# First pair of a two-stage graph kernel: loads in halves, hop 2 in float32, and a reordered end

## What is computed

```python
# first layer
Xw = X @ Wv + bv
sj, si = Xw @ aw[:d, 0], Xw @ aw[d:, 0]
e = leaky_relu(sj[:, None, :] + si[:, :, None] + ab[0], 0.2)
alpha = A * exp(e)
transition = alpha / (sum(alpha, -1, keepdims=True) + 1e-12)
H = 0; Xk = X
for k in range(3):
    H = H + Xk @ Wk[k] + bk[k]
    Xk = transition @ Xk
x = layernorm(x + relu(H))
# second layer
x = layernorm(x + (adj @ x) @ w)
```

## Time and profile before

| what | value |
|---|---|
| median of 3 runs | 272.70 us (272.46 to 272.84) |
| the profiled execution's own time | 272.39 us |
| its span, first to last instruction | 270.6 us |
| TensorE busy (PE) | 264.1 us, 98% |
| TensorE weight loads (PEld) | 246.1 us, 91% |
| VectorE (DVE), ScalarE (ACT), GpSimd (POOL) | 216.7, 193.0, 191.5 us |
| DMA | 34.91 MB, 129 GB/s in the mean |

### The profile page before, as it was taken

One profiled execution on the slowest core, in us unless ns is written; L12 is line 12 of the kernel. 1 busy time (PEld: TensorE's weight loads), 2 busy tenths in 40 slices (PEclk: granted clock), 3 DMA queues, 4 the chain that ended last, 5 costly groups with the idle time before them and its releaser, 6 DMA issues.

```text
span 270.6 us, 6025 instructions
## 1 busy us (share of the span) xinstructions
PE 264.1 (98%) x1890; PEld 246.1 (91%) x1890; DVE 216.7 (80%) x615; ACT 193.0 (71%) x439; POOL 191.5 (71%) x412
## 2 busy tenths in 40 slices
PE   8899999999999999999999999999999999999992
PEld 5899999999999999999999999999999999999991
DVE  0777798888889888888988888988888898788984
ACT  4887767777666777766777766677776667766874
POOL 4665567778877778887777887777788777657533
PEclk9999999999999999999999999999999999999999
DMA  7997486828955488446873484943884457932214
GB/s 242 274 185 94 85 48 218 131 72 147 168 137 159 81 133 117 155 143 156 140 117 80 154 155 137 152 153 51 131 160 100 118 116 75 125 99 78 80 41 155
DMA packets 28342, 34.91 MB, mean 129 GB/s; under 512 B 6803, under 2 KB 16150, under 8 KB 28310
## 3 DMA queue, kind: packets, MB, share of 16 engines
q1 hardware_dynamic: 27888, 34.12, 60.8%
q10 hardware_dynamic: 422, 0.40, 0.4%
HBM read 26.09 MB, written 8.42 MB: 128 GB/s over the span
## 4 chain that ended last, share of the span: by engine, by line
PE 95%; DMA 2%; DVE 1%; SPq 0%; ACT 0%; issue 0%
PE ps_v L1107 31%; PE ps_y L1107 17%; PE ps_out L1107 15%; PE ps_h L1107 11%; PE ps_agg L1271 10%; PE ps_v L1204 3%; PE ps_v L1208 3%; PE ps_v L1206 3%; DMA WY_sb<-Wk_dram 2%; PE ps_agg L1107 2%; DVE last_out_sb L884 0%; PE ps_v L1254 0%; PE ps_h L1245 0%; PE ps_y L1245 0%; PE ps_agg L1254 0%; DVE WY_lo L669 0%
## 5 line engine op out<-in xcount | busy, mean ns | idle before, releaser
L1107 PE MATMUL ps_v<-WX_hi,XT_hi 128*128 128x512 f32 (+1 forms) x132 | 49.0, 371 | 0.0
L1107 PE MATMUL ps_v<-WX_lo,XT_hi 128*128 128x512 f32 (+1 forms) x132 | 48.6, 368 | 0.0
L1107 PE MATMUL ps_v<-WX_hi,XT_lo 128*128 128x512 f32 (+1 forms) x132 | 48.6, 368 | 0.0
L1029 POOL TENSOR_TENSOR XT_lo<-xt,XT_hi 128x512 fp32r<-128x512 f32 x32 | 42.1, 1319 | 6.6 <-ACT XT_hi L426 6.6
L1039 POOL TENSOR_TENSOR alpha<-exps,adjs 128x256 f32<-128x256 f32 x31 | 23.1, 744 | 28.9 <-ACT exps L470 28.8
L1043 POOL TENSOR_TENSOR alpha_lo<-alpha,alpha_hi 128x256 fp32r<-128x256 f32 x31 | 22.8, 735 | 19.4 <-ACT alpha_hi L479 19.4
L1107 PE MATMUL ps_y<-WY_hi,XT_hi 128*128 128x258 f32 x116 | 35.2, 303 | 0.6 <-DVE WY_lo L673 0.6
L503 ACT ACTIVATE y<-res,offset,rstd 128x256 f32<-128x256 f32 x62 | 33.6, 591 | 2.2 <-POOL offset L1005 2.2
L1271 PEld LDWEIGHTS ps_agg<-adjs,y 128*128 128x128 f32 x248 | 32.0, 191 | 2.2
L1271 PE MATMUL ps_agg<-adjs,y 128*128 128x128 f32 x248 | 32.7, 275 | 0.0
L1107 PE MATMUL ps_y<-WY_lo,XT_hi 128*128 128x258 f32 x116 | 32.7, 282 | 0.0
(11 more groups left out here) (179 smaller groups left out, 830.8 us busy)
## 6 DMA issues: line engine op xcount, KB each, us to landing
xt<-xt_dram SPq DMA_DIRECT2D x32, 256.0 KB, 5.7
nodes<-nodes_dram SPq DMA_DIRECT2D x32, 256.0 KB, 5.8
out_dram<-out_sb SPq DMA_DIRECT2D x30, 256.0 KB, 5.3
adjs<-adjs_dram SPq DMA_DIRECT2D x32, 128.0 KB, 5.7
spread<-si_rows_dram SPq DMA_DIRECT2D x29, 128.0 KB, 4.7
si_rows_dram<-scores SPq DMA_DIRECT2D x29, 1.0 KB, 3.9
WvT_sb<-WvT_dram SPq DMA_DIRECT2D x1, 260.0 KB, 3.6
W_sb<-Wk_dram ACTq DMA_DIRECT2D x1, 256.0 KB, 3.3
```

What stands on the lines that cost most here:

```text
L1029: pool.tensor_tensor(XT_lo[k % 7][:].rearrange("p c b i -> p (c b i)"), xt_sb[k % 4][:], XT_hi[k % 7][:].rearrange("p c b i -> p (c b i)") ...
L1107: last = pe.matmul(to, a, b, start=start and n == 0, stop=stop and n == 2, skip_group_check=True)
```

## The change

- X0 and W0 are loaded in two halves each (by chunk of 128 features), with semaphores of their own; first hop 0 goes by chunk instead of by graph, so that it can begin with the first halves. One warm-up product fewer.
- Hop 2 of pair 0 is a whole float32 product of X0 and WY_sb, which has room for the two score columns (`first_hop2`). It waits for W2 and for the columns' copy (`u_ready`), and no longer for high and low parts. `load_xt(4)` waits for it.
- Score weights come behind all of first hop 0, then the sum of biases, which uses ps_v, then the score shift. bk is rounded first on ScalarE's list.
- Hop 2 of pair 1 (`second_hop2`) does the products with X1's high part first, and only then waits for its low part. One graph of hop 2 of pair 2 is moved ahead of `propagate_v2(0)`.
- VectorE's preamble: score columns, bias copy, score shift, low part of W1, low part of W2 with its two columns in one instruction, low part of W0.
- W1, W2 (258 columns) and w lie by partition in DRAM, with runs of 2 KB.
- At the end: the first half of pair 31 is stored ahead of the half of pair 30; the root of graph 0 is taken between the two halves of `late_normalise2(LAST - 2)`; the reciprocal of graph 0 comes ahead of the moments of graph 1.

```diff
@@ SyncE
-                    sp.wait_ge(h_done, 1)
+                    sp.wait_ge(y_done, 1)
...
-            load_xt(0)
+            half = C * PER * P // 2
+            sp.dma_start(xt_sb[0][:, 0:half], xt[0, :, 0:half]).then_inc(first_xt_loaded, DMA)
+            sp.dma_start(xt_sb[0][:, half:2 * half], xt[0, :, half:2 * half]).then_inc(xt_loaded[0], DMA)
...
+            store_last(0)
             sp.wait_ge(late_half_out_ready, 1)
             sp.dma_start(out[LAST - 1, :, 0:D], out_sb[(LAST - 1) % 3][:, 0]).then_inc(last_stored, DMA)
-            for b in range(PER):
-                sp.wait_ge(last_out_ready, b + 1)
-                sp.dma_start(out[LAST, :, b * D:(b + 1) * D], last_out_sb[:, b]).then_inc(last_stored, DMA)
+            store_last(1)
@@ ScalarE
-            act.dma_start(W0_sb[:], Wk[0].rearrange("(c p) n -> p c n", p=P)).then_inc(Wk_loaded[0], DMA)
+            act.dma_start(W0_sb[:, 0], W0[:, 0:D]).then_inc(first_W0_loaded, DMA)
+            act.dma_start(W0_sb[:, 1], W0[:, D:2 * D]).then_inc(Wk_loaded[0], DMA)
...
+            bk_hi_of()
             xt_hi(0)
             wx_hi(0)
             wy_hi()
             wx_hi(1)
-            bk_hi_of()
...
-            late_normalise2(LAST - 2)
+            late_normalise2(LAST - 2, [0])
             last_std2_of(0)
+            late_normalise2(LAST - 2, [1])
@@ VectorE
+            def score_columns():
+                dve.wait_ge(Wk_loaded[2], DMA)
+                dve.wait_ge(u_done, 1)
+                dve.tensor_copy(WY_sb[:, :, D:D + 2], ps_u).then_inc(u_ready, 1)
+                dve.tensor_copy(WY_hi[:, :, D:D + 2], ps_u).then_inc(u_ready, 1)
...
             bk_lo_of()
+            score_columns()
+            bias_of_hops()
             shift_of_scores()
+            first_hop1_low()
+            wy_lo()
             first_hop0_low()
...
+            last_rstd2_of(0)
             last_mom2(1)
-            for b in range(PER):
-                last_normalise2(b)
+            last_normalise2(0)
+            last_rstd2_of(1)
+            last_normalise2(1)
@@ TensorE
+            def first_hop2():
+                pe.wait_ge(Wk_loaded[2], DMA)
+                pe.wait_ge(u_ready, 1)
+                for b in range(PER):
+                    for c in range(C):
+                        last = pe.matmul(hop2(0)[:, b, 0:D + 2], first_X[:, c, b], WY_sb[:, c], start=c == 0,
+                                         stop=c == C - 1, skip_group_check=True)
+                last.then_inc(y_done, 1)
...
-            keep_warm(ps_v[:, 0], 8)
+            keep_warm(ps_v[:, 0], 7)
             first_hop0(0)
+            first_hop0(1)
             score_weights()
-            first_hop0(1)
+            sum_of_biases()
             score_shift()
-            hop2_and_scores(0)
+            first_hop2()
             first_hop1(0)
             pe.wait_ge(identity_ready, 1)
             spread_scores(0)
             first_hop1(1)
-            hop2_and_scores(1)
-            sum_of_biases()
+            second_hop2()
+            hop2_and_scores(2, [0])
             pe.wait_ge(ones_columns_ready, 1)
             propagate_v2(0)
             spread_scores(1)
-            hop2_and_scores(2)
+            hop2_and_scores(2, [1])
             hop2_and_scores(3)
             spread_scores(2)
```

More of the change, by code:

```diff
@@ L16, with resnorm_graph_kernel @@
 NORM_EPS = 1e-5
-def resnorm_graph_kernel(nc, xt, adjs, nodes, WvT, Wk, bk, w, si_rows, out):
+def resnorm_graph_kernel(nc, xt, adjs, nodes, WvT, W0, W1, W2, bk, w, si_rows, out):
     PAIRS = nodes.shape[0]
-    D = w.shape[0]
+    D = bk.shape[1]
     C = D // P
-    HOPS = Wk.shape[0]
+    HOPS = bk.shape[0]
     assert (P, C, HOPS) == (nodes.shape[1], 2, 3)
@@ L361, in load_Wk @@
             def load_Wk(n):
-                to = (W0_sb, W1_sb, WY_sb)[n]
-                sp.dma_start(to[:], Wk[n].rearrange("(c p) n -> p c n", p=P)).then_inc(Wk_loaded[n], DMA)
-            load_xt(0)
+                to, held = ((W1_sb, W1), (WY_sb, W2))[n - 1]
+                sp.dma_start(to[:].rearrange("p c n -> p (c n)"), held).then_inc(Wk_loaded[n], DMA)
+            half = C * PER * P // 2
+            sp.dma_start(xt_sb[0][:, 0:half], xt[0, :, 0:half]).then_inc(first_xt_loaded, DMA)
+            sp.dma_start(xt_sb[0][:, half:2 * half], xt[0, :, half:2 * half]).then_inc(xt_loaded[0], DMA)
             sp.dma_start(WvT_sb[:].rearrange("p c n -> p (c n)"), WvT).then_inc(WvT_loaded, DMA)
@@ L399, in step @@
                     load_adjs(4)
-                    sp.dma_start(w_sb[:], w.rearrange("(c p) n -> p c n", p=P)).then_inc(w_loaded, DMA)
+                    sp.dma_start(w_sb[:].rearrange("p c n -> p (c n)"), w).then_inc(w_loaded, DMA)
                 if there(k - 3):
@@ L405, in _, with store_last @@
                 step(k)
+            def store_last(b):
+                sp.wait_ge(last_out_ready, b + 1)
+                sp.dma_start(out[LAST, :, b * D:(b + 1) * D], last_out_sb[:, b]).then_inc(last_stored, DMA)
+            store_last(0)
             sp.wait_ge(late_half_out_ready, 1)
             sp.dma_start(out[LAST - 1, :, 0:D], out_sb[(LAST - 1) % 3][:, 0]).then_inc(last_stored, DMA)
-            for b in range(PER):
-                sp.wait_ge(last_out_ready, b + 1)
-                sp.dma_start(out[LAST, :, b * D:(b + 1) * D], last_out_sb[:, b]).then_inc(last_stored, DMA)
+            store_last(1)
             for slot in range(3):
@@ L423, in xt_hi @@
             def xt_hi(k):
+                if k == 0:
+                    act.wait_ge(first_xt_loaded, DMA)
                 act.wait_ge(xt_loaded[k % 4], loads(k, 4))
@@ L429, in wx_hi @@
             def wx_hi(n):
+                if n == 0:
+                    act.wait_ge(first_W0_loaded, DMA)
                 act.wait_ge(Wk_loaded[n], DMA)
@@ L509, in aggregate_hi, with late_normalise2 @@
                 act.activation(agg_hi[k % 2][:], agg(k), ACT.Copy).then_inc(agg_hi_ready, 1)
-            def late_normalise2(k):
+            def late_normalise2(k, graphs=range(PER)):
                 act.wait_ge(offset2_ready, k + 1)
                 act.wait_ge(stored[k % 3], loads(k - 3, 3))
-                for b in range(PER):
+                for b in graphs:
                     last = act.activation(out_sb[k % 3][:, b], res2[k % 2][:, b] if k < LAST - 3 else out_place(k)[:, b],
                                           ACT.Identity, bias=offset2[k % 3][:, b:b + 1], scale=rstd2[k % 3][:, b:b + 1])
-                last.then_inc(late_out_ready, 1)
+                if b == PER - 1:
+                    last.then_inc(late_out_ready, 1)
             def late_normalise_from_psum(b):
@@ L1109, in product, with second_hop2 @@
                 return last
+            def first_hop2():
[6 more added lines that the diff above has]
+                last.then_inc(y_done, 1)
+            def second_hop2():
+                pe.wait_ge(WY_ready, 1)
+                pe.wait_ge(shift_ready, 1)
+                pe.wait_ge(xt_hi_ready, 2)
+                for b in range(PER):
+                    for c in range(C):
+                        for n, W in enumerate((WY_hi, WY_lo)):
+                            pe.matmul(hop2(1)[:, b, 0:D + 2], XT_hi[1][:, c, b], W[:, c], start=c == 0 and n == 0,
+                                      stop=False, skip_group_check=True)
+                pe.wait_ge(xt_lo_ready, 2)
+                for b in range(PER):
+                    for c in range(C):
+                        last = pe.matmul(hop2(1)[:, b, 0:D + 2], XT_lo[1][:, c, b], WY_hi[:, c], start=False,
+                                         stop=c == C - 1, skip_group_check=True)
+                last.then_inc(y_done, 1)
             def hop2_and_scores(k, graphs=range(PER)):
-                if k == 0:
-                    pe.wait_ge(WY_ready, 1)
                 pe.wait_ge(xt_lo_ready, k + 1)
[L1117 to L1120, removed]
                 if k > 1:
@@ L1128, in hop2_and_scores, with first_hop0 @@
                     last.then_inc(y_done, 1)
[L1130 to L1136, removed]
+            def first_hop0(c):
+                pe.wait_ge(*((first_xt_loaded, DMA) if c == 0 else (xt_loaded[0], DMA)))
+                pe.wait_ge(*((first_W0_loaded, DMA) if c == 0 else (Wk_loaded[0], DMA)))
+                for b in range(PER):
+                    last = pe.matmul(ps_h[:, b], first_X[:, c, b], W0_sb[:, c], start=b == 0 and c == 0, stop=c == C - 1,
                                      skip_group_check=True)
-                if b == PER - 1:
+                if c == C - 1:
                     last.then_inc(h_done, 1)
@@ L1404, with by_partition @@
         np.concatenate([WvT, np.concatenate(columns).transpose(2, 1, 0)], axis=2).reshape(P, -1))
-    for name in ("Wk", "bk"):
-        arrays[name] = np.ascontiguousarray(inputs["L0_gnn_" + name])
-    arrays["w"] = np.ascontiguousarray(inputs["L1_gnn_w"])
+    def by_partition(m, room=0):
```

(6 more changed lines are left out.)

34 lines of the change are left out of this document (18 added, 16 removed).

## The result

| | kernel before | changed kernel |
|---|---|---|
| median of 18 runs | 272.19 us (271.88 to 272.84) | 273.49 us (272.28 to 274.91) |
| ratio, with 95% interval | 1 | 1.0043 [1.0033, 1.0054] |
| the profiled execution | 272.39 us | 273.62 us |
| its span | 270.6 us | 271.8 us |

A forecast was written before the change was run, and what follows sets the result against it. TensorE, busy throughout the 192 us middle, was taken as the bound, leaving only the two ends. Start 0.1 plus end 0.15 gave 0.25 us less: 272.14 for the profiled execution, 272.45 from the 272.70 median; range 271.8 to 273.0.

The forecast's parts named there:

- If they hold GpSimd all that time, the low part of X1 ends at 10.1 + 1.27 = 11.37: Start: VectorE's W1, W2, W0 subtractions delay GpSimd's low parts of X1 and X2; v2(0) at 13.41, 0.11 us later.
- hop 2 at 7.71: Pair 0's first hop 2 on TensorE starts at 7.71 instead of 7.93 us, behind the score shift loading from 7.30.
- the 0.3 for products that run before the clock rises: TensorE's list before hop 2: about 0.3 us lost as more products run before the clock rises; list ends at 7.45.
- the forecast's path: Before hop 2: GpSimd's product of bv and aw ends at 7.24, the score shift follows, hop 2 starts at 7.71 us.
- The end: Last stores and normalisations reordered: 0.15 us won, bounds 0 and 0.3.
- X4's load: SyncE issues it at about 9.7 instead of 8.04 us, behind first hop 2; costed at nothing.
- the rival on the slow side: X4 lands at 15.4 us, ScalarE starts leaky(1) 1.5 us late, 273.95 us in all; chance 0.12.
- The halves: Splitting the loads of X0 and W0 does nothing for the time; changes the sum by nothing, counted within the 0.46 forecast case.
- the new start: Start up to v2(1): 0.20 us gained in TensorE's list, less 0.11 for the later v2(0), 0.1 us won.
- the very 0.29 that float32 was forecast to cost: Pair 0's hop 2 in float32: eight records, 1.72 us, against twelve at 1.43, 0.29 us more.
- Nothing holds the start: Rival: bk lands early or GpSimd isn't held; hop 2 at 7.45, list to v2(0) at 12.95, 271.9 us; chance 0.30.
- bk lands at 4.7: Rival: bk's load lands late, all 0.5 us later up to v2(0) at 13.9, 272.95 us; chance 0.12.

The follow-up runs named there:

- e10: Changed kernel with GpSimd waiting for W2's low part, W0's low part moved to just before step 0, biases rounded third; median 272.24 us, ratio 0.9996.
- e2: Changed kernel with GpSimd waiting before X1's low part until VectorE has made those of W1, W2 and W0; median 273.03 us, ratio 1.0028.
- e1: Changed kernel with W0's low part moved from VectorE's preamble to just before step 0, behind pair 0's alpha; median 273.28 us, ratio 1.0018.
- e6: Changed kernel run again unedited, on a second chip; six runs, median 273.63 us, ratio 1.0053 to the kernel before, profiled execution 272.10 us.
- e3: Changed kernel with X0 and W0 loaded whole again, one transfer each; median 273.09 us, ratio 1.0021 to the kernel before.
- e8: Same three edits to the changed kernel as e10, run on a second chip; median 272.26 us, ratio 0.9998 to the kernel before.
- e11: Changed kernel with one edit: GpSimd waits for W2's low part before making X1's; median 272.30 us, ratio 1.0003 to the kernel before.
- e5: Changed kernel with the eighth warm-up product put back; median 273.78 us, ratio 1.0046 to the kernel before.
- e9: Changed kernel run a third time unedited, on the chip of e10 and e11; median 273.63 us, ratio 1.0062 to the kernel before.
- e4: Changed kernel with the biases (bk) rounded third on ScalarE's list, behind X0 and W0; median 272.95 us, ratio 1.0004 to the kernel before.
- e7: Kernel before with only the reordered end (stores, root, reciprocal); median 272.19 us, ratio 0.9998 to the kernel before.

## Why the prediction was wrong

**The step that failed** is "If they hold GpSimd all that time, the low part of X1 ends at 10.1 + 1.27 = 11.37". I had the overlap and both lists in it, and let one row decide who pays: in the kernel before GpSimd took 2.19 us while VectorE ran at its own pace. I read that as a rule. In the changed kernel the engines take turns, VectorE stretches to 1.80 and 1.77, and I put nothing on its list; the low part of X1, for which I had over 2.5 us, took 1.27. By the step the price falls on X2's low part and the half of hop 2 that needs it, 0.11 us for v2(0). The price fell on alpha of pair 0, and before it on v2's low part, for which the half of hop 2 also waits; I had named only X2's low part as its input. In numbers: between hop 2 and v2(0) I had 13.41 - 7.71 = 5.70, and it was 6.83. The mis-step is 1.13 us. That the runs without a hold show 5.66 to 5.72 is in part luck: my 5.70 was TensorE's list at 5.50 and 0.20 for GpSimd's hold, where the list alone takes 5.66 (e10).

The Trainium skill, in "GPSIMD Engine Reference", section "1. Specifications", says that GpSimd contends with VectorE instructions with two SBUF inputs, which is what I cited. The traces agree, in both directions (1.27 to 1.77 us on GpSimd, 0.68 to 1.80 on VectorE).

**Mis-sized: hop 2 at 7.71.** It was 8.11. `bv_aw_sum` ended at 7.29 (forecast 7.24) and wasn't the limit: the score shift followed the bias products (7.94 in the chain) without a wait. TensorE's own list was longer. I had 3.14 + 0.24 + 0.3 = 3.68 us from its first weight load to that of hop 2; it took 4.48 (3.60 to 8.08). The term that was too small is the 0.3 for products that run before the clock rises. The weight loads of first hop 0, in the changed kernel, and the second half of them in the kernel before (its first is in the earlier trace rows):

```profile
3.60 2.72 PEld L1181 LDWEIGHTS ps_h<-W_sb,xt 128*128 128x128 f32 x8 [0.61 <-DMA xt<-xt_dram]
```

```profile
6.12 0.73 PEld L1136 LDWEIGHTS ps_h<-W_sb,xt 128*128 128x128 f32 x4
```

That is 2.72 us against 0.94 + 0.73 = 1.67, so 1.05 where I had 0.3. By TensorE's matmuls first hop 0 took 3.03 us here; eight products of the same form, run without a pause, took 1.93 to 3.08 in the experiments. The records of that group reach from 0.38 us, at the 2.4 GHz level, to 0.70, at the 1.2 GHz level, and how many ran at the low level differed by execution: 3.08 us for all in e2 and 1.93 in e1, with the same list on TensorE. In e6 first hop 0 took 2.30 us and the forecast's path held: `bv_aw_sum` ended at 7.25 and the shift followed it. Hop 2 began at 7.55 there, since the weight load of hop 2 came 0.22 us behind that of the shift, where I had 0.41.

**Adding up.** v2(0) was 0.40 + 1.13 late, v2(1) loads at 19.49 where 17.9 was forecast, 1.59 later. The end won 0.25 instead of 0.15. 272.14 + 1.59 - 0.10 = 273.63; the profiled execution had 273.62. The forecast of the median counted from 272.70, a median of three runs; eighteen give 272.19. From there the same sum gives 271.94, and the median's miss is 1.55 us instead of 1.04: a third of it was hidden by luck.

**Right.** The biases' rounding at 4.30 (about 4.2), X0's at 4.63 (4.56). X4's load at 10.13 (9.7), later by hop 2's delay; ScalarE didn't wait for it, so the rival on the slow side named the wrong mechanism. The halves did nothing for the time that e3 could show. Even without the hold the new start gives next to nothing, as the forecast had it (0.1 us): hop 2 begins 0.2 earlier in e8 (7.71 against 7.93), and takes 0.29 longer up to v2(0) (5.66 against 5.37), the very 0.29 that float32 was forecast to cost, as the half of hop 2 that came in (0.73) takes the place of the biases' sum that left (0.66); v2(1) loads at 17.97 in e10 against 17.99. Forecast were 0.25 us below the kernel before; e8, e10 and e11 are 0.08 below to 0.09 above by their medians, within what can be told from no change.

**The rivals.** "Nothing holds the start" (271.9) didn't come: its v2(0) at 12.95 was in no trace; the earliest of the new order was 13.37. "bk lands at 4.7" is real: its rounding began between 4.15 and 5.38 us in the executions with it first, and where it was at 5.20 or later (e1, e5, e11) hop 2 waited 0.7 to 1.0 us for `bv_aw_sum` and came at 8.49 to 8.68; at 4.62 (e9) it waited 0.66 and came at 7.91. On the median it hides: e11, with bk first, has 272.30, e10, with bk third, 272.24, with intervals that overlap. Both have GpSimd's wait; without it bk's place may help to decide which engine begins first (e4); that isn't shown.

**Open.** Why a part of the executions goes the good way isn't settled beyond the order of arrival. By the lists it hangs on when X1's rounding ends and when the score shift is ready, and both move with W2, bk and the clock; no run takes these apart. Nor is who goes next when both wait: in the kernel before VectorE's bk and W0 parts both went ahead of GpSimd's, though GpSimd's had begun between them, which the turns of the changed kernel don't explain. No kernel was tried that has the old start and forces the hold on it.

## What to carry to other kernels

Where a step that is moved brings two engines' subtractions of SBUF operands together, charge both lists, the whole instruction of the other engine each time, and ask what is queued behind each: here one kernel's start was 0.94 us longer (6.83 against 5.89) when GpSimd began 0.03 us ahead than when VectorE began 0.06 us ahead. Look for an engine with slack and make it wait; here one wait on GpSimd gave back 1.33 us. And before moving work off the path, add up the bounding engine's own list up to the next wait: if it is as long as before, the change can gain nothing there and can only lose.

## What the runs showed of the hardware

- Subtractions of VectorE and GpSimd with both operands in SBUF (128x512 float32 in, fp32r out) held each other for whole instructions in these traces: 0.68 us became 1.50 to 1.80 on VectorE, 1.27 became 1.47 to 2.19 on GpSimd. Few partitions don't exempt one: VectorE's 3x256 for bk took 0.77 us beside GpSimd's (e4, e8, e10), 0.41 alone. VectorE's low part of v2, with one operand in PSUM, took 0.67 to 0.69 wherever it stood; in the changed kernel it ran from 12.79 to 13.47 beside a GpSimd subtraction (12.91, 1.29) that wasn't held either.
- The first float32 products ran for different times at the 1.2 GHz level in executions of the same list on TensorE (eight took 1.93 to 3.08 us), while the granted clock read 1.00 in every 1 us window from 3 to 7 us, in the changed kernel, e1 and e6: the records' length (0.38 to 0.70 us) shows the level, the clock column doesn't.
- The small load of the biases, issued third on ScalarE's queue, was there for its rounding between 4.26 and 5.38 us; W2's rounding, where it waited for the landing, began at 6.25 and at 7.04 us with the loads of the kernel before (before, e7), and from 6.26 (e10) to 7.01 with those of the changed one.
